# Wide attention: one product of query and key weights per head instead of two projections

## What is computed

```
q = x @ Wq[h] + bq[h];  k = x @ Wk[h] + bk[h];  v = x @ Wv[h] + bv[h]
p = softmax(q @ k.T / sqrt(D))
x_out += (p @ v) @ Wo[h*D:(h+1)*D]
```

## Time and profile before

| | |
|---|---|
| median of 3 runs | 1398.8 us (1398.34 to 1399.44) |
| the profiled execution | 1406.68 us |
| its span, first to last instruction | 1404.9 us |
| mean granted TensorE clock | 0.884 |
| the wide attention in it | from about 979 to 1241 us of the span |
| a turn | about 62 to 67 us |

### The profile page before, as it was taken

One profiled execution on the slowest core, in us unless ns is written; L12 is line 12 of the kernel. 1 busy time (PEld: TensorE's weight loads), 2 busy tenths in 40 slices (PEclk: granted clock), 3 DMA queues, 4 the chain that ended last, 5 costly groups with the idle time before them and its releaser, 6 DMA issues. The chain is left out here.

```text
span 1404.9 us, 20748 instructions
## 1 busy us (share of the span) xinstructions
PE 1079.1 (77%) x7046; PEld 731.5 (52%) x7046; DVE 713.2 (51%) x1989; ACT 602.5 (43%) x1321; POOL 346.4 (25%) x336
## 2 busy tenths in 40 slices
PE   1467788868886888873588999996989898944677
PEld 1134454545554545542377576674677776832344
DVE  3355566656665667633645211114454445556654
ACT  3134444434553455441643613325545454541355
POOL 4313444444443444234601100013000003013110
PEclk9668899989998999996678989998999999965699
DMA  2745344524462446002000001100000000006640
GB/s 46 138 82 78 66 73 72 100 49 82 74 107 51 73 80 111 10 2 52 10 1 1 15 24 30 30 20 1 8 8 11 4 15 23 1 1 103 100 78 25
DMA packets 76093, 65.33 MB, mean 47 GB/s; under 512 B 11324, under 2 KB 73176, under 8 KB 75992
## 3 DMA queue, kind: packets, MB, share of 16 engines
q1 hardware_dynamic: 72968, 62.09, 24.8%
q0 software_dynamic: 512, 1.05, 0.5%
q10 hardware_dynamic: 2520, 0.99, 0.4%
HBM read 46.83 MB, written 17.27 MB: 46 GB/s over the span
## 5 line engine op out<-in xcount | busy, mean ns | idle before, releaser
L538 DVE TENSOR_REDUCE t_nmax<-banks 128x2 f32<-128x512 f32 x256 | 167.7, 682 | 72.6 <-PE banks L296 71.0
L432 ACT ACTIVATE t_probs<-banks 128x512 f32<-128x512 f32 x256 | 146.6, 597 | 107.2 <-PE banks L320 96.9
L320 PE MATMUL banks<-t_packed 99*128 99x256 bf16 x512 | 107.3, 294 | 34.4 <-issue 17.4
L296 PE MATMUL banks<-t_packed 96*128 96x256 bf16 x512 | 109.9, 302 | 25.4 <-DMA t_packed<-t_qk_parts 25.4
L320 PEld LDWEIGHTS banks<-t_packed 99*128 99x128 bf16 x512 | 45.8, 103 | 86.1 <-issue 63.4
L1824 ACT ACTIVATE l_probs<-banks,l_nmax 128x256 f32<-128x256 f32 x128 | 59.5, 470 | 69.5 <-DVE l_nmax L1850 69.5
L377 PE MATMUL banks<-x1T,wff 128*128 128x512 f32 x128 | 72.2, 675 | 18.5 <-ACT t_oT L442 17.6
L333 PE MATMUL banks<-t_probs,t_v 128*32 128x256 f32 x1024 | 84.7, 411 | 0.1
L1591 ACT ACTIVATE hid<-banks,b 128x512 f32<-128x512 f32 x64 | 43.5, 687 | 81.2 <-PE banks L1529 81.1
L1613 DVE SCALAR_TENSOR_TENSOR acc<-banks,gates,acc 128x128 f32<-128x128 f32 (+1 forms) x72 | 20.0, 342 | 108.8 <-PE banks L1547 108.8
L296 PEld LDWEIGHTS banks<-t_packed 96*128 96x128 bf16 x512 | 52.7, 106 | 42.0 <-DMA t_packed<-t_qk_parts 26.8
(11 more groups left out here) (346 smaller groups left out, 2289.1 us busy)
## 6 DMA issues: line engine op xcount, KB each, us to landing
t_packed<-t_qk_parts SPq DMA_DIRECT2D x192, 128.0 KB, 4.8
t_qk_parts<-t_parts SPq DMA_DIRECT2D x32, 384.0 KB, 6.0
g_packed<-g_qk_parts SPq DMA_DIRECT2D x48, 128.0 KB, 4.6
...
l_wqk<-in_l_qk SPq DMA_DIRECT2D x8, 128.0 KB, 2.0
```

Source lines behind the costliest of these rows:

```text
L296: ins = pe.matmul(m.mbank[:, n % 3, i * S:(i + 1) * S], m.packed[0:MROW, 0, g % PAIRS, h, c + qt * P:c + (qt + 1) * P], m.packed[0:MROW, 1 ...
L320: ins = pe.matmul(m.sbank[:, n % 2, i * S:(i + 1) * S], m.packed[0:MROW + 3, 1, g % PAIRS, h, c + kt * P:c + (kt + 1) * P], m.packed[0:MRO ...
L432: act.activation(m.probs[:, n % 6, :], m.sbank[:, n % 2, :], ACT.Exp).then_inc(sem["probs_ready"], 1)
L538: dve.tensor_reduce(m.nmax[:, b % 2, u // 4, 2 * hp:2 * hp + 2], m.mbank[:, n % 3, :].rearrange("p (i k) -> p i k", i=2), AX.X, ALU.max, n ...
```

## The change

Scores are (x Wq + bq)(x Wk + bk).T. Split, they are (x (Wq Wk.T) + bq Wk.T) @ x.T plus terms with bk, which depend on the query alone. So one projection by the product of both weights replaces two, its bias is bq Wk.T, and the turned input itself stands in for the keys. The terms with bk come out as one number c for each query; the kernel computes it as a column beside the values and forms `shift` = (-maximum - c) + c.

What is done:

- A new item **WT** turns the head's query and key weights by TensorE (two transposes), and ScalarE copies them out as `wT`. ScalarE also writes two broadcasts and a scaled pair of bias columns.
- **VO** grows from two matmuls to six: the product of the weights (`both`), three matmuls with a single moving column, and the two it had. It waits for `wT`. ScalarE copies out three pieces of 129 columns.
- **P** has per group one item "t" of 512 columns (before: two, queries and keys), and the values' item is split into two, 0 and 1, of two 129-column blocks each. All of them, the first too, wait until VO's copies are done.
- `vo`, `bvo` and `vp` have a 129th column beside the values, with a term of each token that comes from a bias.
- In **SC**, the moving operand is `xT` in place of the keys. After the maximum VectorE waits for it by a semaphore and runs two `scalar_tensor_tensor` on one column each, which combine the maximum with the 129th column into `shift`; the exponential waits for `shift_ready` and has `shift` as its bias.
- SP waits only for VO's copies before it loads the next turn's weights.

Two unused names of semaphores are removed in another stage's list as well. The rest of the diff:

```diff
@@ -1642,7 +1642,7 @@
     return {k: np.ascontiguousarray(v.astype(np.float32)) for k, v in arrays.items()}
 
 
-WIDE_SEMS = ("heads_loaded vo_copied lin_ready0 lin_ready1 q_ready v_ready sc_ready max_ready "
+WIDE_SEMS = ("heads_loaded vo_copied weights_turned lin_ready0 lin_ready1 q_ready v_ready sc_ready max_ready shift_ready "
              "exp_ready turned0 turned1 turned_dve turned_act av_ready added rows_ready dve_chain pool_chain act_chain").split()
 WH = 8
 TR = 2
@@ -1666,17 +1666,21 @@
         return stack.enter_context(nc.sbuf_tensor(name, shape, dt))
 
     wqk, wvT, wo, cols = m.l1_wqk, m.l1_wvT, m.l1_wo, m.l1_cols
-    qb = sb("l1_qb", [P, 2])
-    vo, bv_wide, bvo = sb("vo", [P, 2, D]), sb("bv_wide", [P, 2, D]), sb("bvo", [P, 2, D])
-    qk = sb("l1_qk", [P, 2, 2, TOK])
-    vp = sb("vp", [P, 2, TILES, D])
+    scaled = sb("l1_scaled", [P, 2, 2])
+    wT = sb("l1_wT", [P, 2, 2, D])
+    both = sb("l1_both", [P, 2, D + 1])
+    vo, bvo = sb("vo", [P, 2, D + 1]), sb("bvo", [P, 2, D + 1])
+    bv_wide, bq_wide = sb("bv_wide", [P, 2, D]), sb("bq_wide", [P, 2, D])
+    qk = sb("l1_qk", [P, 2, TOK])
+    vp = sb("vp", [P, 2, TILES, D + 1])
     nmax, sums, rsum = sb("l1_nmax", [P, 2, 2]), sb("l1_sums", [P, 4, 2]), sb("l1_rsum", [P, 2, 2])
+    shift = sb("l1_shift", [P, 2, 2])
     probs, pT = sb("l1_probs", [P, 3, 2, S]), sb("l1_pT", [P, TR, 2, S])
     scale = float(D) ** -0.5
 
 
     def project_items(j):
-        return [("VO", j)] + [("P", j, g, i) for g in range(PAIRS) for i in range(3)]
+        return [("WT", j), ("VO", j)] + [("P", j, g, i) for g in range(PAIRS) for i in ("t", 0, 1)]
 
     units = [(j, b) for j in range(2) for b in range(B)]
     order = project_items(0)
@@ -1692,7 +1696,7 @@
             if later and n >= 1:
                 order.append(later.pop(0))
     assert not later
-    uses = [x for x in order if x[0] in ("VO", "P")]
+    uses = [x for x in order if x[0] in ("WT", "VO", "P")]
     turn = {key: (n % 2, n // 2) for n, key in enumerate(uses)}
     at_turn = {v: k for k, v in turn.items()}
     sc, tr, av, lin = banks[:, 0:2, :], banks[:, 2:4, :], banks[:, 4:6, :], banks[:, 6:8, :]
@@ -1700,10 +1704,12 @@
     def turn_of_heads(next_heads):
 
         def read_out(key):
+            if key[0] == "WT":
+                return sem["weights_turned"], key[1] + 1
             if key[0] == "VO":
-                return sem["vo_copied"], 2 * key[1] + 2
+                return sem["vo_copied"], key[1] + 1
             j, g, i = key[1:]
-            return (sem["v_ready"], 4 * j + g + 1) if i == 2 else (sem["q_ready"], 8 * j + 2 * g + i + 1)
+            return (sem["q_ready"], 4 * j + g + 1) if i == "t" else (sem["v_ready"], 8 * j + 2 * g + i + 1)
 
         def ready(eng, key):
             eng.wait_ge(sem["lin_ready0"] if turn[key][0] == 0 else sem["lin_ready1"], turn[key][1] + 1)
@@ -1714,8 +1720,7 @@
                 if next_heads is not None:
                     for j in range(2):
 
-                        sp.wait_ge(sem["q_ready"], 8 * (j + 1))
-                        sp.wait_ge(sem["vo_copied"], 2 * j + 2)
+                        sp.wait_ge(sem["vo_copied"], j + 1)
                         for dst, src in head_loads(t, m, j, next_heads[j]):
                             sp.dma_start(dst, src).then_inc(sem["heads_loaded"], 16)
                     sp.wait_ge(sem["heads_loaded"], 16 * 2 * HEAD_LOADS)
@@ -1743,33 +1748,45 @@
                     ins.then_inc(sem["lin_ready0"] if turn[key][0] == 0 else sem["lin_ready1"], 1)
 
                 for item in order:
-                    if item[0] == "VO":
+                    if item[0] == "WT":
                         j = item[1]
                         bank = use(item)
-                        pe.matmul(bank[:, 0:D], wvT[:, j, :], wo[:, j, :], start=True, stop=True)
+                        for i in range(2):
+                            ins = pe.transpose(bank[:, i * D:(i + 1) * D], wqk[:, j, i, :], m.ident[:, :])
+                        filled(item, ins)
+                    elif item[0] == "VO":
+                        j = item[1]
+                        bank = use(item)
+                        pe.wait_ge(sem["weights_turned"], j + 1)
+                        pe.matmul(bank[:, 0:D], wT[:, j, 0, :], wT[:, j, 1, :], start=True, stop=True)
                         pe.wait_ge(sem["rows_ready"], j + 1)
-                        filled(item, pe.matmul(bank[:, D:2 * D], bv_wide[:, j, :], wo[:, j, :], start=True, stop=True))
+                        pe.matmul(bank[:, D:D + 1], wT[:, j, 1, :], scaled[:, j, 0:1], start=True, stop=True)
+                        pe.matmul(bank[:, 129:257], wvT[:, j, :], wo[:, j, :], start=True, stop=True)
+                        pe.matmul(bank[:, 257:258], wT[:, j, 0, :], scaled[:, j, 1:2], start=True, stop=True)
+                        pe.matmul(bank[:, 258:386], bv_wide[:, j, :], wo[:, j, :], start=True, stop=True)
+                        filled(item, pe.matmul(bank[:, 386:387], bq_wide[:, j, :], scaled[:, j, 1:2], start=True, stop=True))
                     elif item[0] == "P":
                         _, j, g, i = item
                         bank = use(item)
-                        if i < 2:
-                            ins = pe.matmul(bank, wqk[:, j, i, :], m.xT[:, g * PW:(g + 1) * PW], start=True, stop=True)
+                        if g == 0:
+                            pe.wait_ge(sem["vo_copied"], j + 1)
+                        if i == "t":
+                            ins = pe.matmul(bank, both[:, j, 0:D], m.xT[:, g * PW:(g + 1) * PW], start=True, stop=True)
                         else:
-                            if g == 0:
-                                pe.wait_ge(sem["vo_copied"], 2 * j + 2)
-                            for a in range(4):
-                                c = g * PW + a * P
-                                ins = pe.matmul(bank[:, a * P:(a + 1) * P], m.xT[:, c:c + P], vo[:, j, :], start=True, stop=True)
+                            for a in range(2):
+                                c = g * PW + (2 * i + a) * P
+                                ins = pe.matmul(bank[:, a * (D + 1):(a + 1) * (D + 1)], m.xT[:, c:c + P], vo[:, j, :],
+                                                start=True, stop=True)
                         filled(item, ins)
                     elif item[0] == "SC":
                         n = item[1]
                         j, b = units[n]
-                        pe.wait_ge(sem["q_ready"], 8 * j + 2 * (b // 2) + 2)
+                        pe.wait_ge(sem["q_ready"], 4 * j + b // 2 + 1)
                         if n >= 2:
                             pe.wait_ge(sem["exp_ready"], n - 1)
                         for qt in range(2):
                             c = b * S + qt * P
-                            ins = pe.matmul(sc[:, n % 2, qt * S:(qt + 1) * S], qk[:, j, 0, c:c + P], qk[:, j, 1, b * S:(b + 1) * S],
+                            ins = pe.matmul(sc[:, n % 2, qt * S:(qt + 1) * S], qk[:, j, c:c + P], m.xT[:, b * S:(b + 1) * S],
                                             start=True, stop=True)
                         ins.then_inc(sem["sc_ready"], 1)
                     elif item[0] == "T":
@@ -1786,43 +1803,52 @@
                         n = item[1]
                         j, b = units[n]
                         pe.wait_ge(sem["turned_act"] if n % 2 else sem["turned_dve"], n // 2 + 1)
-                        pe.wait_ge(sem["v_ready"], 4 * j + b // 2 + 1)
+                        pe.wait_ge(sem["v_ready"], 8 * j + b + 1)
                         if n >= 2:
                             pe.wait_ge(sem["added"], n - 1)
                         for qt in range(2):
                             for kt in range(2):
                                 ins = pe.matmul(av[:, n % 2, qt * D:(qt + 1) * D], pT[:, n % TR, kt, qt * P:(qt + 1) * P],
-                                                vp[:, j, 2 * b + kt, :], start=(kt == 0), stop=(kt == 1))
+                                                vp[:, j, 2 * b + kt, 0:D], start=(kt == 0), stop=(kt == 1))
                         ins.then_inc(sem["av_ready"], 1)
 
             @block.scalar
             def _(act):
                 chain = Link(act, sem["act_chain"])
                 for item in order:
-                    if item[0] == "VO":
+                    if item[0] == "WT":
                         j = item[1]
 
-                        act.activation(bv_wide[:, j, :], cols[:, j, 2:3].broadcast_to([P, D]), ACT.Copy).then_inc(sem["rows_ready"], 1)
-                        chain.step(act.mul(qb[:, j:j + 1], cols[:, j, 0:1], scale))
+                        act.activation(bv_wide[:, j, :], cols[:, j, 2:3].broadcast_to([P, D]), ACT.Copy)
+                        act.activation(bq_wide[:, j, :], cols[:, j, 0:1].broadcast_to([P, D]), ACT.Copy)
+                        act.mul(scaled[:, j, :], cols[:, j, 0:2], scale).then_inc(sem["rows_ready"], 1)
                         ready(act, item)
```

(42 more changed lines are left out.)

4 lines of the change are left out of this document (2 added, 2 removed).

## The result

The changed kernel's median is 1412.1 us over 20 runs (1403.1 to 1420.4), that of the kernel before beside it on the same chip 1400.1 us over 20 runs (1396.6 to 1410.8, and one run of 1558.8). The ratio is 1.0086, 95% interval 1.0067 to 1.0105: 9 to 15 us slower, some 12 us. The forecast was 5.1 us slower, 1403.9 us, with a range up to 1409.5. The profiled execution took 1413.76 us, 7.1 more than the one before.

A forecast was written before the change was run, and what follows sets the result against it. Bound by the slackless chain scores, maximum, exponential, transpose together with TensorE's own work. First stretch 3.6 lost, second 4.7 gained, third 6.2 lost: 5.1 us slower, 1403.9 us from a median of 1398.8; range 1397.5 to 1409.5.

The forecast's parts named there:

- first stretch: Part of each wide-attention turn with the first head's projections alone in TensorE's queue: 3.6 us lost in all (1.2 to 9).
- third stretches: End of each turn, units run alone: D paid four times, 1.56 us a turn, 6.2 us lost (4.5 to 7.2).
- The bottleneck: Where units run alone, the chain scores, maximum, exponential, transpose has no slack; it and TensorE's own work bind together.
- rivals 1 and 3: 1: D is absorbed, 1397.7 us, chance 0.14; 3: TensorE's work alone binds, 18.6 us gained, 1380.2 us, chance 0.08.
- D: Time the two new VectorE instructions put between maximum and exponential: 0.39 us, bounds 0.28 and 0.45.
- Second stretch: Part of each turn with the second head's projections between units: 1.2 us gained a turn, 4.7 in all (3.5 to 5.9).
- D is hidden here: In the second stretch a mixed unit takes 3.1 us or more, so TensorE never waits for the exponentials.
- Sum 12.6, against 11.79: 0.8 us lost: Last turn's first stretch: hand-over, then three projection groups, reach the first scores after 12.6 us; before, 11.79.
- TensorE held the full clock over 2.5 us of rest: Observation on turn four before the change, in the clock rival; a fall to 1.2 GHz there would cost about 1.9 us.
- rival 2: New hand-over rests drop TensorE's clock: 1.9 us in turn four, 1.1 in each other; 5.2 more, 1409.1 us, chance 0.16.

The follow-up runs named there:

- the series: Four kernels: changed without the pair, changed with one copy instead, before with the pair alone, changed; third stretch 18.35, 19.04, 19.75, 20.03 us.
- before_pair: The kernel before with only the pair of one-column VectorE instructions added between maximum and exponential, reading a constant column; ratio 1.005 to the kernel before.

## Why the prediction was wrong

The forecast was 8.2 us short: 1.3 because the kernel before stood at 1400.1 us and not at 1398.8, the rest in the change. Of the 5.4 us by which the first profile's stage exceeds the forecast, 3.5 lie in the last turn's first stretch, 0.8 in the other three, 0.8 in the third stretches and 0.3 in the second ones.

**The bottleneck.** Right. Every row of the series says that maximum, exponential and transposes have no slack, and rivals 1 and 3 are out. TensorE's busy time fell by 4.8 us and bought nothing as the change stands.

**D and the third stretch: right in kind, 0.07 us short.** The start at 0.04 us after the maximum, the 0.13 us between the two and the 0.22 us of each gave 0.39, and before_pair measures 0.38. Each instruction takes 0.22 us (0.35 for both, 0.13 apart). An estimate by the formula of the Trainium skill ("VectorE: DVE Perf Modes", section "The TRN2 errata"), which is for a tensor-tensor operation, gives 0.16; the measured 0.22 decides. What the sum lacked are 0.07 us ahead of the first instruction, most likely the second wait. D is 0.46, the upper bound having been 0.45; four of them were forecast and 3.7 measured; 1.69 us a turn instead of 1.56. The last turn has 0.27 more. Its timeline has one unit in which the second one-column instruction comes late, with nothing in the profile that would hold it:

```profile
1228.81 0.22 DVE L1885 SCALAR_TENSOR_TENSOR l_shift<-l_nmax,vp 128x1 f32<-128x1 f32 x1
...
1229.21 0.22 DVE L1885 SCALAR_TENSOR_TENSOR l_shift<-l_nmax,vp 128x1 f32<-128x1 f32 x1 [0.18 <-issue]
```

It starts 0.40 us after the first instead of 0.13. In all five profiles with this pair and this column the same instruction is late by the same amount (last third stretch 20.29 to 20.31), and in none of the others does the last stretch differ. In all, 7.0 us instead of 6.2.

**Second stretch: right sum.** 26.82 us instead of 26.7, 4.4 us gained instead of 4.7. The product item at full clock, in the last turn's timeline:

```profile
1200.53 0.30 PEld L1761 LDWEIGHTS banks<-l_wT 128*128 128x128 f32 x2 [1.23 <-issue]
...
1201.64 0.30 PEld L1767 LDWEIGHTS banks<-l_scaled,bq_wide 128*128 128x128 f32 x2
...
1201.86 0.73 PEld L1789 LDWEIGHTS banks<-xT,l_qk 128*128 128x128 f32 x4
```

Twelve passes take 1.33 us, one-column passes as long as the others; 1.28 was forecast. The next scores come 6.64 us into the stretch (1195.22 to 1201.86), where 6.6 was forecast. "D is hidden here" was false: without the pair the stretch is 0.59 us shorter, so the rest of the change gains 1.7 us a turn and not 1.2. The two errors nearly cancel, and that the sum came out right is luck.

**First stretch: the step that failed.** "Sum 12.6, against 11.79: 0.8 us lost" took the full clock for the last turn. At full clock the sum is right: 12.65 and 12.64 us with the rests filled. But TensorE ran at the 1.2 GHz level through much of it, and the stretch lost 4.3, 1.9 and 4.3 us in three profiles. The reason given, "TensorE held the full clock over 2.5 us of rest", was a reading of one turn of four, and of one pattern of work around that rest, which the change altered. In the second and third turn of that same profile TensorE rests for as long ahead of the turn, and the clock falls 1.6 and 0.2 us behind its first load (0.96 over 1047 to 1048, 0.89 over 1112 to 1113, then 0.50). In turns one to three the forecast was 2.8 us lost; measured are 3.6, 2.8 and 3.6. All first stretches together lose 7.9, 4.7 and 7.9 us instead of 3.6.

**The sum.** The three profiles give 10.5, 9.0 and 10.5 us in the stage, the ratios 12.0, 11.1 and 10.2 us of 1400 with intervals that begin at 9.4, 7.3 and 7.8. That is near rival 2, the clock, which had the kernel 10.3 us slower, with nearly the mechanism that was named for it: the lower level in the last turn cost up to 3.5 us beyond the forecast, not 1.9, and the first three turns up to 0.8 more, not 3.3. Its chance, 0.16, was too low: the reason against the forecast stood in its own rows, 0.77, 0.88 and 0.78.
